# Two-layer graph network on one core: layer 0's node update spread over two loop iterations, and waits of GpSimd for its own gathers

## What is computed

```python
h = relu(layernorm(x))
agg = segment_sum(h[src], dst, 12500)
x = x + agg @ W_rel.T + b_rel + h @ W_root.T                     # layer 0
h = relu(layernorm(x))
edge_weights = silu(edge_attr @ We1 + be1) @ We2 + be2           # 50 -> 128 -> 128
agg = segment_sum(h[src] * edge_weights, dst, 12500)
x = x + silu(agg @ Wn1 + bn1) @ Wn2 + bn2                        # layer 1
```

## Time and profile before

| | us |
|---|---|
| median of 3 runs | 4783.59 |
| lowest, highest | 4771.58, 4814.32 |
| profiled execution, its own time | 4752.23 |
| its span, first to last instruction | 4750.4 |

### The profile page before, as it was taken

One profiled execution on the slowest core, in us unless ns is written; L12 is line 12 of the kernel. 1 busy time (PEld: TensorE's weight loads), 2 busy tenths in 40 slices (PEclk: granted clock), 3 DMA queues, 4 the chain that ended last, 5 costly groups with the idle time before them and its releaser, 6 DMA issues.

```text
span 4750.4 us, 29563 instructions
## 1 busy us (share of the span) xinstructions
PE 2158.6 (45%) x7600; PEld 1272.9 (27%) x7600; DVE 2216.7 (47%) x2541; ACT 739.0 (16%) x1263; POOL 2999.1 (63%) x3135
## 2 busy tenths in 40 slices
PE   1112111111111111111347777777777777778778
PEld 0111001010101101011124444444444444444444
DVE  5889577575875759567612222222222222222222
ACT  2400000000000000000112222222222222222222
POOL 6376757577575776757366666666666666666663
PEclk9975555555555555555567778777778777778788
DMA  4212212122221222212122222222222222222222
GB/s 118 80 52 59 59 47 64 46 59 58 53 60 46 62 53 56 59 45 66 49 60 65 65 67 66 65 68 66 64 65 66 66 64 69 67 65 66 65 64 63
DMA packets 230578, 296.56 MB, mean 62 GB/s; under 512 B 68964, under 2 KB 160278, under 8 KB 230433
## 3 DMA queue, kind: packets, MB, share of 16 engines
q0 software_dynamic: 100096, 205.20, 16.7%
q10 hardware_dynamic: 61378, 60.59, 4.7%
q1 hardware_dynamic: 69086, 30.60, 2.4%
HBM read 269.68 MB, written 26.48 MB: 62 GB/s over the span
## 4 chain that ended last, share of the span: by engine, by line
DVE 31%; another core or an unknown queue 24%; PE 24%; issue 16%; ACT 2%; DVEq 2%; POOL 0%; DMA 0%; ACTq 0%; SPq 0%; POOLq 0%
DVE wide L894 14%; PE wide L459 7%; PE wide L454 6%; PE seg L415 6%; DVE xs L900 4%; DVE onehot L900 3%; DVE ys L900 3%; PE ew_b L465 2%; PE ew_a L465 2%; DVE onehot L883 1%; DVEq L911 1%; DVE onehot L865 1%; DVE agg L907 1%; PE node L473 1%
## 5 line engine op out<-in xcount | busy, mean ns | idle before, releaser
L353 POOL DMA_INDIRECT rows<-h_rows,idx x3060 | 2926.7, 956 | 1666.4 <-issue 1023.2
L894 DVE TENSOR_TENSOR wide<-rows,consts_ps 128x1536 f32<-128x1536 f32 (+1 forms) x414 | 691.7, 1671 | 44.1 <-issue 32.6
L415 PE MATMUL seg<-onehot,rows 128*128 128x128 f32 x3128 | 538.4, 329 | 372.7 <-DVE agg L924 281.3
L1051 DVE TENSOR_TENSOR rows<-ew_a,rows 128x512 f32<-128x512 f32 x207 | 142.8, 690 | 1104.2 <-remote 508.7
L459 PE MATMUL wide<-hidden,we_sb 128*128 128x512 f32 x784 | 549.1, 789 | 191.4 <-ACT hidden L647 187.9
L415 PEld LDWEIGHTS seg<-onehot,rows 128*128 128x128 f32 x3128 | 491.9, 240 | 411.5 <-DVE agg L924 310.2
L647 ACT ACTIVATE hidden<-wide,be_col 128x512 f32<-128x512 f32 x393 | 270.0, 687 | 1555.0 <-remote 934.8
L1051 DVE TENSOR_TENSOR rows<-ew_b,rows 128x512 f32<-128x512 f32 x184 | 126.7, 689 | 565.8 <-PE ew_b L465 190.2
L405 PE MATMUL seg<-onehot 128*128 128x128 f32 x138 | 37.8, 447 | 667.3 <-DVE agg L907 477.4
L652 ACT ACTIVATE agg<-wide,be_col 128x512 f32<-128x512 f32 x392 | 268.3, 684 | 293.9 <-PE wide L459 146.0
L454 PE MATMUL wide<-ef_a,we_sb 50*128 50x512 f32 x418 | 274.9, 743 | 29.5 <-DMA ef_a<-ef_blocks 25.6
(11 more groups left out here) (174 smaller groups left out, 1688.5 us busy)
## 6 DMA issues: line engine op xcount, KB each, us to landing
rows<-h_rows,idx POOLq DMA_INDIRECT x3060
ef_a<-ef_blocks ACTq DMA_DIRECT2D x70, 300.0 KB
node_work<-ef_blocks ACTq DMA_DIRECT2D x47, 300.0 KB
xs<-x SPq DMA_DIRECT2D x40, 256.0 KB
ys<-y_rows SPq DMA_DIRECT2D x26, 256.0 KB
out<-xs ACTq DMA_DIRECT2D x26, 256.0 KB
y_rows<-ys ACTq DMA_DIRECT2D x25, 256.0 KB
h_rows<-node_work ACTq DMA_DIRECT2D x23, 256.0 KB
```

The costliest lines, as they stand in the source:

```text
L353: pool.indirect_dma_start(out=rows[:, u, t, :], out_offset=None, in_=table, in_offset=bass.IndirectOffsetOnAxis(ap=idx[:, j:j + 1], axis=0 ...
L415: mm = pe.matmul(seg_ps[:, 0:P], rows[:, u, t, :], onehot[:, g % 2, k * TB + t, :], start=(k == 0 and t == 0), stop=(last and t == TB - 1))
L894: v.tensor_tensor(picked[:, 0:tiles, :], rows[:, first:first + tiles // TB, :, :].rearrange("p k t f -> p (k t) f"), run_mask[:, r, first ...
L1051: v.tensor_tensor(rows[:, u, :, :], ew, rows[:, u, :, :], ALU.mult).then_inc(s_msg, 1)
```

## The change

The node update of layer 0 reaches over two iterations: TensorE's `product` stands ahead of group 4, `turned_back` ahead of group 1 of the next iteration; VectorE does `x1` behind group 2 of the next iteration, `node_shift` behind 3, y behind 4. ScalarE does the earlier update's bias and root ahead of the current `turned`, its later steps behind. The bias goes to `node_work[:, 0, :]` (`biased`), as `aggT` would be written again by then. SyncE loads indices ahead of `node_x`. GpSimd waits for the landing of the group just issued ahead of groups 2 and 4 and at the end of each iteration of layer 0 (`STOPS[0]`), and ahead of group 3 and at the end in layer 1 (`STOPS[1]`).

```diff
+STOPS = ([2, 4, 6], [3, 6])
+        biased = [node_work[:, 0, :], *aggT[1:]]
...
                 with sp.Fori(1, ITERS) as it:
+                    next_idx(0, p * ITERS + it, it)
                     node_x([loop_group(it)], p * (ITERS - 1) + it - 1)
-                    next_idx(0, p * ITERS + it, it)
...
                     if g == HALF // GB:
                         hold(pool, s_idx_b, loads * 16 + 16)
+                    if g in STOPS[layer]:
+                        hold(pool, s_rows[layer][g - 1], landed(i, g - 1))
...
+                if G in STOPS[layer]:
+                    hold(pool, s_rows[layer][G - 1], landed(i, G - 1))
...
-                with pe.Fori(1, ITERS) as it:
-                    i = p * ITERS + it
-                    steps = node_update0(p * (ITERS - 1) + it - 1, 0)
+                def edges0(it, first):
+                    n = p * (ITERS - 1) + it - 1
                     for g in range(G):
-                        if g in steps:
-                            steps[g]()
-                        run_sums(i, g)
+                        if g == 1 and not first:
+                            node_update0(n - 1, 0)[4]()
+                        if g == 4:
+                            node_update0(n, 0)[3]()
+                        run_sums(p * ITERS + it, g)
+                edges0(1, True)
+                with pe.Fori(2, ITERS) as it:
+                    edges0(it, False)
+                node_update0((p + 1) * (ITERS - 1) - 1, 0)[4]()
...
-                    nc.scalar.activation(aggT[r], node_t[r][:, :], ACT.Identity, bias=b_rel_col[:, :]).then_inc(s_nbias, 1)
+                    nc.scalar.activation(biased[r], node_t[r][:, :], ACT.Identity, bias=b_rel_col[:, :]).then_inc(s_nbias, 1)
...
+                node_steps(1)[0]()
+                with act.Fori(2, ITERS) as it:
+                    steps, earlier = node_steps(it), node_steps(it - 1)
+                    earlier[1]()
+                    earlier[2]()
+                    steps[0]()
+                    earlier[3]()
+                    earlier[4]()
+                    earlier[5]()
+                last = node_steps(ITERS - 1)
+                for k in (1, 2, 3, 4, 5):
+                    last[k]()
...
-                    if g == 0 and not first:
+                    if g == 2 and not first:
+                        earlier[3]()
+                    if g == 3 and not first:
                         earlier[4]()
-                    if g == 1 and not first:
+                    if g == 4 and not first:
                         earlier[5]()
-                    if g == G - 1:
-                        steps[3]()
```

More of the change, by code:

```diff
@@ L429, in turned_back @@
                     for t in range(TB):
-                        tr = pe.transpose(node_o[r][:, t * D:(t + 1) * D], aggT[r][:, t * P:(t + 1) * P], ident[:, :])
+                        tr = pe.transpose(node_o[r][:, t * D:(t + 1) * D], biased[r][:, t * P:(t + 1) * P], ident[:, :])
                     tr.then_inc(s_no, 1)
@@ L612, in _, with node_steps @@
                         edge_std(p * U, u + 1)
-                with act.Fori(1, ITERS) as it:
+                def node_steps(it):
                     n = p * (ITERS - 1) + it - 1
-                    side_by_side([node_update0(loop_group(it), n, 0, (p * ITERS + it) * G + LAG, n + 1)])
+                    return node_update0(loop_group(it), n, 0, (p * ITERS + it) * G + LAG, n + 1)
+                node_steps(1)[0]()
[10 more added lines that the diff above has]
+                    last[k]()
             hold(act, s_acc[0], passes0 * N_SUMS + LAG)
@@ L968, in node_rest @@
                 steps = node_update0(n, 0, n + 1)
+                steps[3]()
                 steps[4]()
@@ L979, in edges0 @@
                 landed_last = dve.snap(landed(i, G - 1))
-                steps, earlier = node_update0(n, 0, n + 1), node_update0(n - 1, 0, n)
+                earlier = node_update0(n - 1, 0, n)
                 for g in range(G):
```

## The result

The changed kernel took 4828.7 us (median), the kernel before beside it 4792.4: ratio 1.0077, 95% interval 1.0055 to 1.0100. The forecast was 4708 with a range up to 4790. The profiled executions differ by more, 4847.6 against 4752.2, since the one of before lies under its median and the one of after above. I compare stages in them, and totals in the medians.

The account below looks back on a forecast made before the run. No engine was full; GpSimd's gather pace, 84.9 us per iteration, was the floor, with pauses above it. Terms -45 (layer 0), -22 (tail), +3 and -12 (layer 1) gave -76: 4708 against the median 4783.6, range 4600 to 4790.

Parts of the forecast that it names:

- what is late next is GpSimd's own pace: Layer 0: with index-load pauses gone, gathers set the pace, 84.9 us plus stops, 92.9 us per iteration.
- Cost 0: Layer 0's spread node update: adds no loop instruction, hides lateness of 30 us and more, VectorE can wait 20 us; cost 0.
- GpSimd's pauses come from `x1`, which waits for TensorE's late releases: Layer 0: pauses of 26.5 to 28.7 us, one in three iterations, traced through index loads and y to a late `x1`.
- Index loads: Layer 0, SyncE: loads ahead of `node_x` no longer stand behind y, removing the 28 us pause, some 9 us per iteration.
- Three stops: 2.6 us each: Layer 0, GpSimd: each landing wait of 2.9 us replaces a 0.30 gap, costing 2.6 us, three 7.8 per iteration.
- Layer 0, -45 us at the last gather: Layer 0: 21 iterations of 92.9 us instead of 1995.5 us in all; last gather 45 us earlier.
- Tail, -22: End of layer 0: VectorE follows closely, last sum 10.5 us behind the last gather instead of 34.1; together -22 us.
- Layer 1's stops, +3: Layer 1: two stops fall mostly inside GpSimd's existing pauses ahead of groups 3 and 0, adding 3 us in all.
- Layer 1's first iteration, -12: Layer 1's first iteration: a stop midway through its 68-gather burst lets one more group through, -12 us (0 to -15).
- The stops may not bring TensorE's releases in time: Rival: `x1` still waits 27 us each time; 4730, or about 4858 with 27 in each iteration; no separate chance.
- no change: Rival: stops of 4.2 us eat what the index loads give, total 4786; chance 0.18, both ways.
- slower: Rival: landings come late behind a burst, a stop taking 7.1 us, total 4969; chance 0.12.

Follow-up runs that it names:

- e1: Changed kernel without any GpSimd stops (spread node update and moved index loads remain): 4058.6 us where the kernel before took 4055.4, ratio 1.0007.
- e4: Kernel before plus layer 0's three stops, node update not spread: 4198.5 us where the kernel before took 4055.4, ratio 1.0352.
- e10: Changed kernel without any stops, on a chip where the kernel before took 4773.1 us: 4833.3 us, ratio 1.0124.
- e15: The changed kernel itself, timed again where the kernel before took 4825.5 us: 4835.8 us, ratio 1.0029.
- e13: Changed kernel with layer 0's three stops only, layer 1's removed: 4838.0 us where the kernel before took 4825.5, ratio 1.0015.
- e12: Changed kernel without stops, plus 72 small ScalarE copies per layer 0 iteration from the third on: 4970.4 us, kernel before 4773.1, ratio 1.0389.
- e9: Changed kernel without stops, second of three matmuls in each run_sums left out: 4701.0 us, kernel before 4748.4, ratio 0.9903.
- e7: Changed kernel, stops kept, with the second of three matmuls in each run_sums left out: 4364.1 us, ratio 1.0746 to the kernel before.

## Why the prediction was wrong

It forecast 4708 from a sum of -76 us; the medians say +36. The step that failed is the slack that it gave VectorE: "it can also wait some 20 us per iteration" before GpSimd would notice, hence "what is late next is GpSimd's own pace" and, for the spread node update, "Cost 0". The runs showed VectorE without slack. It took 66.6 us of work, 26.1 of waiting for TensorE and 3.1 of small gaps in each iteration of before, which is the 95.8; after, the waiting is 30.3 and the iteration 98.2. Point by point:

- *GpSimd's pauses come from `x1`, which waits for TensorE's late releases.* Right for this kind of chip, and the runs on the other kind show it from the far side: with prompt releases e1 and e4, one of either order, have no such pause, and the kernel before takes 4055 us. But the rows were not read to the end. "It waits for one thing, `x1`" left out the window adds, 95.6 us in 18 iterations. There are six pauses of 26.5 to 28.7 us, not five. And a seventh, 16.6 us at 366.11, ends with VectorE's L894 and not with an index load: a first sign that GpSimd meets VectorE itself.
- *Index loads.* They wait as little as forecast: no long pause ends with one. The 9 us per iteration that this was to give did not come.
- *"What is late next is GpSimd's own pace."* Here the working failed. The 10 us of pauses were not SyncE's order but VectorE's time. With the index loads out of the way GpSimd met VectorE at `s_pick`, one iteration further on. No run moves the index loads alone; this rests on the sums above.
- *Node update spread: "Cost 0".* It rested on two more groups of slack for "bias and transposes" hiding "lateness of 30 us and more". The bias has them. The transposes' release does not: two groups of sums lie between it and `x1`, before and after. The lateness was 43.8 us at the bias and 59.1 at `x1`, each `x1` waited up to 26.5 us, and VectorE waited for 30.3 us per iteration (545.5 in 18). On a late chip the spread takes 3.3 us more per iteration (e10 against the first chip's profile) and costs 1.2%, and on a prompt one it costs nothing (e1, 1.0007). Whether the node update or the index loads' place does it, no run tells.
- *Three stops: 2.6 us each.* Right in size: 2.4 to 2.5 and 3.0 with the 0.30 in them, 7.0 us for the three where I had 7.8. Wrong in use: they were to let TensorE's releases catch up, and the release of the transposes came through neither of the two stops inside the 59.1. What they do on a late chip is to stand for a part of GpSimd's pauses (one of 21 us in four iterations in place of 41 in three).
- *Layer 0, -45 us at the last gather.* Measured +55 in the profiles (2315.91 against 2260.47): 8 before iteration 4, 43 in iterations 4 to 21, 4 in the last.
- *Tail, -22.* -2: VectorE did not follow closely.
- *Layer 1's stops, +3.* No cost that e15 against e13 shows, though the first two profiles differ by 40 us behind layer 0. Layer 1's first iteration, -12: 107.2 us in both kernels, nothing.

Of the rivals, the last one came nearest: "The stops may not bring TensorE's releases in time", with 27 us of waiting in each iteration, 4858. Its condition, "It needs TensorE's releases as late behind 24 gathers as behind 140", is what the trace of after shows. The waiting is 30.3 us, but only 16.1 of it at `x1`, where the rival had all 27; the rest is the window adds'. It was given no chance of its own, half of it counted with "no change" and half with "slower", because I took one prompt release behind 5 us of gathering for proof that a short pause is enough; it came after 28 us of pause, which had cleared everything.

The rule of the Trainium skill that I set aside (TensorE: Matmul & The Clock Gate, "The cost: per-tile semaphore tail") held on the prompt chips, where VectorE's waits name no release of TensorE at all and the stops were cost alone, as it would have it: +7.4%. On the late ones it does not hold.

## What to carry to other kernels

When an engine waits for releases that come late, add its waits to its busy time before you call it free: here 66 + 26 of 96 us, and 3 in small gaps, left VectorE no slack, and the runs in which it waited longer (e10, e12) were slower. Check the slack of each wait by itself: the change gave the bias two more groups and left `x1` with the two it had. A short wait placed to "let others catch up" must be measured against how long a pause it takes: releases came at once behind pauses of 20 us, and up to 59 us late across stops of 2.4. And time a change on more than one chip: beside the spread, these stops are worth about -1% on one kind and +7% on the other.

## What the runs showed of the hardware

- Chips differ by 17 to 19% on the same kernel: 4055 and 4062 us on two, 4748 to 4826 on the others. Within one set of runs the times of the kernel before lie within 0.2% on a prompt chip and 1.2% on a late one, and one late chip gave 4748 in one set and 4826 in the next. Busy times of the engines per iteration are alike (VectorE 67.1 and 66.6 us); what differs is how soon a release or an own next instruction comes while GpSimd gathers without a break.
- On the late kind, gathers at 1.25 us each go on for two to three iterations and then something is held back: gathers to 1.40 us (e9), ScalarE's 0.20 us copies to one per 1.40 us (e12), TensorE's releases by 26 to 59 us. In the one place looked at, VectorE's instructions show no such spacing: at 851.43 and 851.64 in the changed kernel two follow within 0.21 us. Pauses of 20 to 28 us end it; one stop of 2.4 does not.
- The semaphore updates that the traces hold tell the two kinds apart. e1 to e7 have 60,939 to 61,018 each, the late chips' traces 16,343 to 18,930, though the records of instructions are all there (29,554 in e1 and in e10, the same kernel). Of the 50,048 updates that the landings of the gathers make, 16 each, e1 has 49,994 and the kernel before 11,077. While the others are late these records come at one pace: 314 from 980 to 1200 us in the kernel before, 261 from 700 to 880 in the changed one, 134 from 1480 to 1575 in e9, which is one in 0.70, 0.69 and 0.71 us. Behind the pause that ends at 941.08 there are 99 from 940 to 950. In layer 0 of e1 it is 14.4 in each us. ScalarE's copies stand once, twice or three times 0.70 us apart.
- What it is that piles up is therefore narrowed down but not shown. It is not the load of the DMA engines, which per iteration is the same: a share of 0.21 of 95.8 us (before) and 0.24 of 85.2 (e1), 20 us both. The Trainium skill (NOTIFIC — the notification-queue block, "Overflow: three behaviours, one of which stalls the engine") names one shared path that can hold engines back, that of the records which they write while they run: its inner stages hold up the producer when they are full. Records at a fixed pace, and more instructions making the lateness worse, would fit it. VectorE's close instructions fit it less, and by that rule the inner stages hold up the producer rather than lose a record, while here seven in ten updates are missing. Whether the records are the cause or only suffer from it, and whether a late chip would be late without them, no run here tests, since each comes with its records; that stays open.
